# Layer 0's accumulators through copies by ScalarE, the first expert tile turned among shared products, two down products placed in the tail

## The reference

```python
x = _layernorm(x + _L0_attn_ref(x, ...))
x = _layernorm(x + _L0_ffn_ref(x, ...))
x = _layernorm(x + _L1_attn_ref(x, ...))
x = _layernorm(x + _L1_ffn_ref(x, ...))
```

```python
q, k, v = rms_norm(x @ q_kernel), rms_norm(x @ k_kernel), x @ v_kernel
...
logits = jnp.einsum('btkgh,bskh->bkgts', q * scale, k)
probs = softmax(logits)
return (probs applied to v).reshape(B, T, N * H) @ out_kernel
```

## Time and profile before

| what | value |
|---|---|
| median of 3 runs | 892.38 us (888.31 to 895.56) |
| the profiled execution's own time | 892.14 us |
| its span, first to last instruction | 890.1 us |
| TensorE busy (matmul) in the span | 786.6 us, 88% |
| ScalarE, VectorE busy | 352.7 us, 455.5 us |
| mean granted TensorE clock | 0.948 of full speed |

### The profile page before, as it was taken

The page is one execution under the profiler, slowest core; times in us unless marked ns, Lnnn a source line. Parts: engine busy times, 40 slices in busy tenths (PEclk is TensorE's granted clock), DMA queues, the critical chain, the costliest instruction groups (busy, mean ns, idle before and its releaser), DMA issues. The chain is left out here.

```text
span 890.1 us, 11488 instructions
## 1 busy us (share of the span) xinstructions
PE 786.6 (88%) x3907; PEld 416.0 (47%) x3908; DVE 455.5 (51%) x1213; ACT 352.7 (40%) x549; POOL 97.5 (11%) x111
## 2 busy tenths in 40 slices
PE   5599999998898889999998688879898899989886
PEld 3222434444335556666655334434454444543675
DVE  2743753563335622222236794786855675653353
ACT  3388775774571111111124113444421533146130
POOL 0000000000000011111541101222000100112000
PEclk9689999999999999999988698989999999999998
DMA  6558035015017061111114780004600181000000
GB/s 208 158 179 271 31 84 166 1 48 154 0 50 235 13 174 42 47 47 41 41 62 130 213 258 15 2 8 131 170 1 2 39 238 33 1 2 24 13 12 25
DMA packets 51582, 75.01 MB, mean 84 GB/s; under 512 B 7607, under 2 KB 44763, under 8 KB 49227
## 3 DMA queue, kind: packets, MB, share of 16 engines
q1 hardware_dynamic: 49660, 69.26, 25.8%
q0 software_dynamic: 1872, 5.11, 2.1%
HBM read 46.57 MB, written 27.66 MB: 83 GB/s over the span
## 5 line engine op out<-in xcount | busy, mean ns | idle before, releaser
L616 PE MATMUL ps<-arena 128*128 128x256 f32 (+5 forms) x1084 | 332.7, 456 | 20.1 <-DVE arena L1205 4.6
L616 PEld LDWEIGHTS ps<-arena 128*128 128x128 f32 (+1 forms) x1084 | 203.1, 197 | 111.1 <-issue 70.2
L921 ACT ACTIVATE arena<-ps 128x1024 f32<-128x1024 f32 x128 | 124.0, 1021 | 53.7 <-PE ps L650 53.2
L1010 ACT ACTIVATE arena<-ps 128x1024 f32<-128x1024 f32 (+3 forms) x128 | 82.6, 702 | 110.2 <-PE ps L854 110.1
L1371 DVE TENSOR_REDUCE arena<-ps 128x1 f32<-128x512 f32 (+3 forms) x176 | 101.1, 634 | 38.2 <-PE ps L832 37.4
L721 PE MATMUL ps<-arena 128*128 x184 | 86.6, 594 | 1.2 <-DVE arena L1276 1.2
L664 PE MATMUL ps<-arena 128*32 128x512 f32 x512 | 70.6, 621 | 10.1 <-DVE arena L1097 9.0
L830 PE MATMUL ps<-arena 96*128 96x128 bf16 (+3 forms) x256 | 65.7, 313 | 13.9 <-DVE arena L1371 8.5
L650 PE MATMUL ps<-arena 96*128 96x512 bf16 x256 | 72.4, 397 | 6.0 <-DMA arena<-q_stacks_dram 4.0
L1455 POOL TENSOR_SCALAR_AFFINE_SELECT arena<-arena 128x512 f32<-128x512 f32 x64 | 42.2, 660 | 278.4 <-ACT arena L1010 278.4
L1414 POOL DMA_INDIRECT arena<-xs_dram,arena x23 | 21.9, 951 | 411.3 <-DVE arena L1270 306.4
(11 more groups left out here) (143 smaller groups left out, 668.8 us busy)
## 6 DMA issues: line engine op xcount, KB each, us to landing
arena<-stacks_dram SPq DMA_DIRECT2D x16, 768.0 KB, 6.1
arena<-in_gate_up_proj SPq DMA_DIRECT2D x8, 1024.0 KB, 9.3
arena<-q_stacks_dram SPq DMA_DIRECT2D x8, 768.0 KB, 5.9
stacks_dram<-arena SPq DMA_DIRECT2D x16, 384.0 KB, 3.0
arena<-in_down_proj SPq DMA_DIRECT2D x8, 512.0 KB, 8.8
stacks_dram<-arena SPq DMA_DIRECT2D x16, 256.0 KB, 3.4
q_stacks_dram<-arena SPq DMA_DIRECT2D x8, 384.0 KB, 4.1
yg_dram<-arena SPq DMA_DIRECT2D x23, 128.0 KB, 1.7
```

The lines of the kernel that those rows point to most:

```text
L616: last = nc.tensor.matmul(dst[0:rows, lo:hi], a, w, start=(n == 0), stop=(n == len(pairs) - 1))
L921: nc.scalar.activation(probs[:, 2 * p:2 * p + 2, :], ps[:, 2 * p:2 * p + 2, :], ACT.Exp)\
L1010: nc.scalar.activation(cprobs[:, i % 2, 2 * p:2 * p + 2, P * kt:S], ps[:, 2 * p:2 * p + 2, P * kt:S], ACT.Exp).then_inc(exp_done[p], 1)
```

## The change

In layer 0, ScalarE copies bank 4 to `o_sb` in the fourth slot of each head group, as its part of `attP`, and that copy frees the bank. `F` then transposes from `o_sb` in SBUF, through `a_t` or an older part of `o_sb`. In the strings F0, F1, F2 stand one slot later (Q3, T2, Su2 and others that shared their slots stay). Layer 1 keeps VectorE's transpose from PSUM (`cF`).

In the end stage, the turn of the first expert tile is part of step D1 of batch 3, ahead of its products on TensorE, and VectorE's copy of it ahead of D1's addition. The wait for the last shared steps follows the first tile's gate and up products and the second tile's turn.

In layer 1, the down products cD2 and cD3 of batch 2 leave the last slot of `C_LAST` and stand in `C_END`: cD2 between cF3 and cP0, cD3 between cP1 and cN0. cO0 of batch 2 stands alone in the last slot but one.

```diff
-A_FIRST = """.rw0 |  |  |  | .F0 | +T0 | >X0 | +T1 | .F1 +T2 |  | >X1 |  | .F2 |  |  |  |"""
+A_FIRST = """.rw0 | | | | | +T0 .F0 | >X0 | +T1 | +T2 | .F1 | >X1 | | | .F2 | | |"""
...
--cH6 | .cF2 -cH7 | -cD0 | -cD1 -cO0 | -cD2 -cD3 |"""
-C_END = """-cF3 -cP0 -cP1 -cN0 -cI0 -cI1 -cI2 -cI3 -cI4 -cN1 -cI5 -cI6 -cI7 =cO1 -cI8 -cI9
+-cH6 | .cF2 -cH7 | -cD0 | -cD1 | -cO0 |"""
+C_END = """-cF3 =cD2 -cP0 -cP1 =cD3 -cN0 -cI0 -cI1 -cI2 -cI3 -cI4 -cN1 -cI5 -cI6 -cI7 =cO1 -cI8 -cI9
...
                 elif n == "D":
+                    if b == B - 1 and i == 1:
+                        xg_turn(0, 0, 0, 0)
                     for f in range(NF):
                         consumed(pe, ("Su", b, f))
...
             pe.wait_ge(s_dn, 16 * E)
-            for last in (("Su", B - 1, NF - 1), ("D", B - 1, 0), ("D", B - 1, 1)):
-                consumed(pe, last)
             e0 = expert(0)
-            xg_turn(0, 0, 0, 0)
             gate_or_up(0, 0, 0, 0, e0)
             gate_or_up(0, 0, 0, 1, e0)
             xg_turn(1, 1, 1, 0)
...
+            for last in (("Su", B - 1, NF - 1), ("D", B - 1, 0), ("D", B - 1, 1)):
+                consumed(pe, last)
             tile_body(0, 0, 0, 1)
...
+                elif n == "attP" and i % NT == NT - 1:
+                    act.wait_ge(pv_done, head0 * b + i + 1)
+                    if b and i == NT - 1:
+
+                        act.wait_ge(at_ready, 2 * b)
+                    nc.scalar.activation(o_sb[:, i // NT, :], ps[:, 4, :], copy).then_inc(o_evac, 1)
...
-            def rows_of(group, turned, rows_t, norm, r, ready, n):
-
-                hg = group % HG
-                v.wait_ge(pv_done, NT * (group + 1))
+            def rows_of(hg, turned, rows_t, norm, r, ready, n):
+
                 by_q = turned.rearrange("p (k r) -> p k r", r=2 * HD)
-                nc.vector.transpose(turned, ps[:, 4, :]).then_inc(o_evac, 1)
-                v.wait_ge(o_evac, group + 1)
                 link(nc.vector.reciprocal(r, by_q[:, :, HD]))
...
                 elif n == "F":
-                    rows_of(HG * b + i, o_sb[:, i, :], a_t, attn, rden, at_ready, 2 * b)
+                    v.wait_ge(o_evac, HG * b + i + 1)
+                    turned = a_t[:, 1, :] if i == 0 else o_sb[:, i - 1, :]
+                    link(nc.vector.transpose(turned, o_sb[:, i, :]))
+                    rows_of(i, turned, a_t, attn, rden, at_ready, 2 * b)
...
                 elif n == "D":
+                    if b == B - 1 and i == 1:
+                        xgt_tile(0, 0, 0)
                     rows = x_sb[:, NT * b + 2 * i:NT * b + 2 * i + 2, :]
...
-            xgt_tile(0, 0, 0)
             xgt_tile(1, 1, 1)
...
                 elif n == "cF":
-                    rows_of(HG * (B + b) + i, co_sb[:, i, :], c_a_t, cattn, rden, cat_ready, 2 * b)
+                    v.wait_ge(pv_done, head0 * B + headc * b + NT * (i + 1))
+                    nc.vector.transpose(co_sb[:, i, :], ps[:, 4, :]).then_inc(o_evac, 1)
+                    v.wait_ge(o_evac, HG * (B + b) + i + 1)
+                    rows_of(i, co_sb[:, i, :], c_a_t, cattn, rden, cat_ready, 2 * b)
```

More of the change, by code:

```diff
@@ L71 @@
 A_START = """X0 X1 Q0 Q1 Q2 Q3 rp0 rp1 +X0 +X1 V0 T0 rp2 T1 T2 +Q0 +Q1 +Q2 +Q3 +rp0 +rp1 +rp2"""
-A_FIRST = """.rw0 |  |  |  | .F0 | +T0 | >X0 | +T1 | .F1 +T2 |  | >X1 |  | .F2 |  |  |  |"""
[L73 to L77, removed]
+A_FIRST = """.rw0 | | | | | +T0 .F0 | >X0 | +T1 | +T2 | .F1 | >X1 | | | .F2 | | |"""
+A_SECOND = """-F3 .V0 +Q0 | -P0 | -P1 +Q1 | +Q2 | +Q3 | .F0 +rp0 +rp1 +rp2 | -N0 -N1 | -R0 -Sg0 | -Sg1
+-Sg2 -Sg3 | +T0 -Su0 .F1 | +T1 +T2 | -Su1 -Su2 | -Su3 | .F2 | -D0 | -D1 |"""
+A_THIRD = """-F3 .V0 +X0 +X1 | +Q0 -P0 | -P1 | +Q1 | +Q2 | .F0 +Q3 +rp0 +rp1 +rp2 | -N0 -N1 | | -Sg0
+-Sg1 -R0 -Sg2 -Sg3 | -Su0 .F1 | +T0 | +T1 +T2 -Su1 | -Su2 | -Su3 .F2 | -D0 | -D1 |"""
+A_LAST = """.V0 -F3 | | -P0 | -P1 | | .F0 | -N0 | -N1 | -R0 | .F1 | | | | .F2 | | |"""
 A_END = """-F3 =Sg0 =Sg1 -P0 -P1 =Sg2 =Sg3 =Su0 =Su1 -N0 -N1 =Su2 -R0 =Su3 =D0 =D1 RK0 -Sg0 -Sg1
@@ L620, in cols, with xg_turn @@
                 return slice(P * t, P * (t + 1))
+            def xg_turn(j, half, n, i):
+                pe.wait_ge(xg_in[half], 16 * (i + 1))
+                if n:
+                    pe.wait_ge(xgt_sb, j)
+                for c in range(2):
+                    last = nc.tensor.transpose(ps[:, 4, cols(c)], xg[:, half, cols(c)], ident)
+                last.then_inc(xgt_ps, 1)
             pe.wait_ge(s_ident, 16)
@@ L704, in _ @@
                     last.then_inc(full_of(step), 1)
[L707 to L713, removed]
             def gate_or_up(j, half, n, up, e):
@@ L1105, in rows_of, with xgt_tile @@
                     v.wait_ge(ready, n + hg // 2 + 1)
+            def xgt_tile(j, half, n):
+                v.wait_ge(xgt_ps, j + 1)
+                if n >= 2:
+                    v.wait_ge(u_full, j - 1)
+                nc.vector.tensor_copy(xg_t[:, half, :, :].rearrange("p c n -> p (c n)"), ps[:, 4, 0:C]).then_inc(xgt_sb, 1)
             nc.vector.memset(ones, 1.0).then_inc(s_ones, 1)
@@ L1270, in _ @@
                     nc.vector.tensor_tensor(ids, src[:, 24:24 + MT], id_hi, ALU.add).then_inc(free_of(step), 1)
[L1272 to L1276, removed]
             def h_tile(j, half, n):
```

## The result

| | before | after |
|---|---|---|
| median (4 runs each, same chip) | 890.44 us (888.31 to 895.56) | 881.36 us (879.10 to 883.43) |
| ratio, 95% interval | | 0.9885 (0.9857 to 0.9913) |
| profiled execution's own time | 892.14 us | 880.45 us |
| mean granted clock | 0.948 | 0.958 |

The change is 1.15% faster: 9.1 us by the medians, 11.7 us by the two profiled executions. The forecast was 884.5 us, in a range of 878.5 to 890.5. A fourth run of before, 888.50 us, moves its median from the 892.38 that the prediction had to 890.44.

The account below looks back on a forecast made before the run. TensorE is busy nearly throughout, so its idle time was taken to count. Gains of 4.35 (layer 0), 2.35 (expert tile) and 0.95 us (tail), 7.65 in all, off 892.14 gave 884.5 us, range 878.5 to 890.5.

Parts of the forecast that it names:

- Layer 0: Layer 0's attention: three waits for VectorE's transpose go, 8.35 us, less losses from the copies; net 4.35 us gained.
- The three gains: Layer 0's waits in batch 0 slot 8, batch 2 slot 12, batch 3 slot 4: 1.2, 1.9 and 5.25 us gained.
- The edges: Layer 0, batches 0 to 1 and 1 to 2: V waits behind F3, behind the copy; 1.15 and 0.75 us lost.
- slot 7 of batch 1: Layer 0: the copy delays ScalarE's work before the table load, so T0 waits for a bank; 0.6 us lost.
- Light slots, where the copy shows: Layer 0, batch 0 slots 3 and 11, batch 3 slot 11: each copy costs 0.5 us, 1.5 us lost.
- The transposes on VectorE stay: Layer 0: VectorE transposes from SBUF, a slot later, where nothing waits for them; no loss counted.
- The expert tile: End stage: gate products follow D1 directly, at 318.27 instead of 320.63; 2.35 us gained.
- The tail: Layer 1's end: cD2 and cD3 take 7.17 us; cD3 is in the way twice, so 0.95 us gained.
- the upper bound: Tail: clock stays up behind the idle time before cP0, chain 1.55 us shorter; 2.5 us gained.
- the lower bound: Tail: clock also falls in the new wait before cI1, products lose about 1.7 us; tail loses 0.75 us.
- Of the rivals, 1: Whole kernel: copies cost nothing and the clock stays up in the tail; 13.2 us gained, 879 us; chance 0.25.
- Rival 3: Layer 0: ScalarE becomes the bound, all 16 copies cost about 1.0 us each; slower, 896.5 us; chance 0.05.

Follow-up runs that it names:

- copies_alone: The changed kernel with the expert tile's and the tail's parts undone, leaving only layer 0's part; median 883.55 us, ratio to before 0.9924.
- tail_alone: The kernel before with only cD2 and cD3 of batch 2 moved into the tail; median 890.61 us, ratio to before 0.9992.

## Why the prediction was right, point by point

**Layer 0: mis-sized, 4.35 predicted, 6.24 measured.** The three gains were 1.65 net of slot 7's copy (predicted 1.2), 2.23 (1.9) and 5.55 us (5.25), 1.1 us more than said. The edges lost 1.06 and 0.63 us (1.15 and 0.75; 84.1 + 2.59 is 86.69 and not 86.75, so that the first should have read 1.1), slot 7 of batch 1 0.51 (0.6). The term that was most off is "Light slots, where the copy shows: ... 3 x 0.5 = 1.5 us": slot 3 of batch 0 cost 0.35 us, slot 11 0.13, and slot 11 of batch 3 moved the next exponentials by 0.34 us, which were made up within two slots. The reading, not tested by itself, is that ScalarE's idle time, counted by me as 0.33 us in two slots, pays back over more of them; only with a second copy did slot 11 cost its full 0.62 us. "The transposes on VectorE stay ... a slot later, where nothing waits for them" was wrong at one place: F1 of batch 1 cost 0.5 us, which putting it back gave back.

**The expert tile: right.** 2.35 predicted, 2.72 in the whole, 2.8 alone (7.20 us from D0 to the gate, where `copies_alone` and `tail_alone`, in the old order, take 10.02). The turn between the products takes 0.22 us of TensorE's time (310.46 to 310.68), not 0.43, and D0 and D1 take 6.99 us from start to start (306.93 to 310.46, 310.68 to 314.14), not the row's 7.14.

**The tail: the steps right, 0.5 to 0.6 where 0.95 was said.** cD3 was in the way twice as predicted, and the wait before cI1 ended with its addition. The prediction let the clock fall at cP0. In the profiled execution it stayed up there (the 1.55 us of the upper bound) and fell before cI1 (the 1.7 us of the lower bound). From the start of the last 16 products ahead of the attention's last sums to N1, three executions of the old tail took 28.1 us on average (28.01, 28.00, 28.31), the seven of the changed one 27.5 (26.86 to 28.61). In `copies_alone` cP0 and cP1 took 3.72 us where the row of before has 5.41, so the old tail has it both ways too:

```profile
833.18 3.72 PE L616 MATMUL ps<-arena 128*128 128x256 f32 x16 [2.47 <-DVE arena L1106]
```

The prediction set beside this the rule of the Trainium skill (TensorE: Matmul & The Clock Gate, "The HAM clock gate") that the watch over the activity runs freely. Three falls in seven at cP0 agree with it; the gain of 1.7 us that the prediction worked out from it did not come. Each of the seven has a fall at one of the two places: four behind the wait before cI1 (N1 27.5 us after that start), two at cP0 (26.9), one at both (28.6). The prediction had no term for the clock falling at the later wait when it had stayed up at the earlier one.

**The sum.** 7.65 predicted; 9.5 by the local steps, 9.1 and 9.9 us by medians (the second from all 8 runs of after, 881.9, and 52 of before, 891.8). That the terms behind layer 0 came out 0.4 us above (experts) and 0.4 us below (tail) their forecasts and cancel is luck; the 1.9 us that are left are layer 0's. The profiled execution that the sum started from lay at the median of before, so its total did not bias the forecast, though it had one fall fewer in layer 0 than the other two traces with the old layer 0; the profiled execution of after was one with few falls. The measured 881.36 us lies in the range and 3.1 us below the forecast, but on the far side of 1%: the prediction gave 0.55 to a change of under 1% and 0.42 to faster. Of the rivals, 1 was the nearest with 13.2 us, as the copies cost less than taken, but edges and tail spoke against it. Rival 3 needed 0.73 us per copy: even the second copy, which has less cover, costs 0.41.

## What to carry to other kernels

Compare two traces place by place, from a marker that both have (here the exponentials of each slot), before believing the difference of two totals: of 11.7 us here 9.5 were gained where the change acts, and the rest came from falls of the clock elsewhere. Look also whether a wait that goes had a fall behind it: that gain is real, but one trace does not tell its size. When a copy is moved to another engine, look for its price in the slots where that engine has no idle time and at the edges where something is queued behind it (here 1.06 and 0.63 us); put what is waited for (V) ahead of what is not (F3). Work put into a wait can move the wait: here cD2 and cD3 left 2.47 us before cI1, and cD3 put earlier left 2.96 us before N0. Look for such a new idle time, at the next step that needs the same engine or bank, before counting the gain.

## What the runs showed of the hardware

One and the same program had between 600 and 780 us no fall of TensorE's clock in one execution and three in another (granted clock 1.00 and 0.97), each worth 1.7 us, at waits of the same length, and before 891 us spread over 7 us (888.2 to 895.6 in 52 runs). In two kernels with the same instructions up to the tail, in step to 0.1 us, the falls still differed (one and three). Behind the same idle time of 2.28 us before cP0 the clock fell in three of seven executions, behind 2.34 us in the end stage in six of thirteen; behind 4.24 us in layer 0 it fell in all three that have this wait. What decides which idle time is followed by a fall was not found here; the runs show that it isn't the instructions alone, and that taking a wait away took its falls away in layer 0.
